# A fused LoRA, attention and mixture kernel on one core: x first among the loads, zero products in waits, adapter products in half-height tiles, the last tile in two parts

## The reference, cut to what matters

```python
# 1: dense layer with a LoRA adapter (rank 16) chosen by sequence; * 2.0
base_out = jnp.einsum('bti,oi->bto', x, W) + b
lora_h = jnp.einsum('bti,bir->btr', x, lora_As[adapter_mapping])
y = base_out + jnp.einsum('btr,bro->bto', lora_h, lora_Bs[adapter_mapping]) * SCALING
# 2: attention, 32 query heads of 16 on 8 key/value groups, rotary, causal
q, k, v = y @ Wq, y @ Wk, y @ Wv            # split in heads
q, k = _apply_rope(q, cos_t, sin_t), _apply_rope(k, cos_t, sin_t)
weights = jax.nn.softmax(jnp.where(causal, -jnp.inf, scores) / 4.0, axis=-1)
x1 = x + (weights_times_v @ Wo)             # the residual is added outside the layer
# 3: dense layer with a rank-32 adapter chosen by sequence (5 labels); * 0.5
z = x1 @ W2.T + (x1 @ A2[label]) @ lora_B_w.T * 0.5
# 4: mixture of 4 rank-16 experts, top 2 gates
gates = softmax over the two largest of z @ router_w.T
out = x1 + sum over experts of gate * ((z @ A.T) @ B) * 4
```

## Time and profile before

| | us |
|---|---|
| median of 3 runs (169.52 to 172.09) | 171.23 |
| the profiled execution's own time | 172.04 |
| its span, first to last instruction | 170.4 |
| TensorE busy | 146.8 (86%) |
| DVE, ACT, POOL busy | 96.2, 78.8, 76.7 |
| mean granted clock of TensorE | 0.984 |

### The profile page before, as it was taken

One profiled execution on the slowest core, in us unless ns is written; L12 is line 12 of the kernel. 1 busy time (PEld: TensorE's weight loads), 2 busy tenths in 40 slices (PEclk: granted clock), 3 DMA queues, 4 the chain that ended last, 5 costly groups with the idle time before them and its releaser, 6 DMA issues.

```text
span 170.4 us, 4660 instructions
## 1 busy us (share of the span) xinstructions
PE 146.8 (86%) x1792; PEld 126.9 (74%) x1792; DVE 96.2 (56%) x215; ACT 78.8 (46%) x158; POOL 76.7 (45%) x78
## 2 busy tenths in 40 slices
PE   0049899999898998999999998999999899888942
PEld 0048749988887996888899996888997778666620
DVE  0045265170559853545829872676964388756583
ACT  2235072794246987133347961215498341833110
POOL 0360054039694999226221684447209845720000
PEclk9999999999999999999999999999999999999985
DMA  5998867632122201224302361002432100623114
GB/s 169 287 294 241 349 251 258 229 65 59 46 81 61 65 2 44 58 64 133 100 0 81 119 199 61 0 0 89 144 119 102 65 0 2 188 100 129 37 62 185
DMA packets 15143, 19.32 MB, mean 113 GB/s; under 512 B 5714, under 2 KB 10066, under 8 KB 14866
## 3 DMA queue, kind: packets, MB, share of 16 engines
q1 hardware_dynamic: 14146, 16.94, 30.5%
q10 hardware_dynamic: 720, 1.84, 3.3%
q0 software_dynamic: 256, 0.26, 0.6%
HBM read 12.47 MB, written 2.10 MB: 86 GB/s over the span
## 4 chain that ended last, share of the span: by engine, by line
PE 49%; POOL 17%; ACT 12%; DVE 9%; DMA 6%; issue 4%; SPq 1%; POOLq 1%; DVEq 0%
PE bank L928 34%; PE bank L954 7%; DMA xF<-xt 6%; ACT qx L302 5%; POOL ex L514 5%; PE bank L983 4%; PE bank L936 4%; POOL qr L545 3%; POOL Kbd L551 2%; POOL qkc L526 2%; POOL kr L539 2%; ACT kx L302 2%; POOL sm L519 1%; POOL qks L533 1%; DVE cTl L676 1%
## 5 line engine op out<-in xcount | busy, mean ns | idle before, releaser
L519 POOL TENSOR_TENSOR sm<-sm,mx 128x512 f32<-128x512 f32 x16 | 17.1, 1073 | 25.1 <-DVE mx L699 24.9
L954 PE MATMUL bank<-xTh,WTh 128*128 128x256 f32 x64 | 16.9, 304 | 10.9 <-ACT xTh L302 10.9
L514 POOL TENSOR_TENSOR ex<-ex,ri 128x512 f32<-128x512 f32 x16 | 17.7, 1106 | 13.1 <-DVE ri L705 13.1
L302 ACT COPY qx<-bank 32x512 f32<-32x512 f32 x32 | 18.5, 577 | 5.7 <-PE bank L928 5.3
L954 PEld LDWEIGHTS bank<-xTh,WTh 128*128 128x128 f32 x64 | 11.8, 205 | 11.3 <-issue 11.0
L694 DVE TENSOR_TENSOR sm<-bank,mixed 128x512 f32<-128x512 f32 x16 | 10.6, 675 | 16.6 <-PE bank L928 16.6
L368 ACT ACTIVATE ex<-sm 128x512 f32<-128x512 f32 x16 | 10.2, 635 | 18.7 <-POOL sm L519 18.5
L928 PE MATMUL bank<-yTh,Wqh 128*128 128x256 f32 x64 | 18.3, 285 | 0.0
L928 PE MATMUL bank<-yTh,Wql 128*128 128x256 f32 x64 | 17.9, 280 | 0.0
L928 PE MATMUL bank<-yTl,Wqh 128*128 128x256 f32 x64 | 17.9, 280 | 0.0
L954 PE MATMUL bank<-xTl,WTh 128*128 128x256 f32 x64 | 16.6, 293 | 0.4 <-DVE xTl L643 0.4
(11 more groups left out here) (97 smaller groups left out, 364.1 us busy)
## 6 DMA issues: line engine op xcount, KB each, us to landing
RS<-RL SPq DMA_DIRECT2D x32, 136.0 KB, 2.0
xF<-xt SPq DMA_DIRECT2D x8, 256.0 KB, 6.2
xres<-xn SPq DMA_DIRECT2D x8, 256.0 KB, 3.2
out<-x SPq DMA_DIRECT2D x8, 256.0 KB, 2.1
Wqn<-wq ACTq DMA_DIRECT2D x2, 512.0 KB, 9.4
Wn<-w SPq DMA_DIRECT2D x1, 1024.0 KB, 4.9
Wqn<-wo SPq DMA_DIRECT2D x1, 1024.0 KB, 4.8
x<-small SPq DMA_DIRECT2D x1, 904.0 KB, 6.9
```

What stands on the lines that cost most here:

```text
L302: return nc.scalar.copy(dst, src)
L514: nc.gpsimd.tensor_tensor(ex[:, j], ex[:, j], ri[:, j, :, None].broadcast_to((P, 2 * NG, T)), ALU.mult).then_inc(normed, 1)
L519: nc.gpsimd.tensor_tensor(sm[:, j % 2], sm[:, j % 2], mx[:, j, :, None].broadcast_to((P, 2 * NG, T)), ALU.subtract).then_inc(shifted, 1)
L954: nc.tensor.matmul(FR[c // 2][:, (c % 2) * TOK:(c % 2 + 1) * TOK], WT[u][:, k, P * c:P * (c + 1)], xT[r][:, k], start=first, stop=False, s ...
```

## The change

What it does, in the order of the kernel:

- **Loads.** Half 0 of x is SP's first transfer, before `mix`; half 1 follows `mix`. `ids` is loaded by POOL. ACT loads W blocks 0, 1, 2; it issues the halves of Wq later, between its casts (the first after `w_high(1)`, the second after `wq_high(0)`). W2 and Wkv are issued ahead of `small` (the router and label weights), and the tables for group 1 (`next_slots(1)`) and 2 directly behind Wo; `load_x(3)` stands ahead of `load_x(2)`, and both behind `next_slots(2)`.
- **First product.** `y_first` goes by contraction block k: the high products of block k as soon as it is there, the low ones (`y_first_low`) a step later; `adapter_in(0)` stands ahead of the last low block.
- **Folding.** `fold_router` and `fold_label_b` stand behind three q tiles and a kv tile, no longer ahead of them.
- **Zero products.** `keep_clock(n, dst)` is n float32 products of a 128x128 tile of zeros (`still`, set by DVE) with itself: 10 ahead of the first product, 6 between `y_adapter` and the first q tile, 6 near the end. Nothing reads them.
- **Adapter output.** `hT` is block-diagonal: rows 0 to 63 have values only in token columns 0 to 127, rows 64 to 127 only in columns 128 to 255. `y_adapter` now makes 8 products of 64 rows and 128 columns where it made 4 of 128 rows and 256 columns. Products that follow each other take the two halves of the rows in turn and write to two banks; between the two calls stands a wait on the new semaphore `y_half`, and `y_ps` is counted in the second call only.
- **Last tile in two parts.** For the last token tile `project_cols` makes columns 0 to 255 and 256 to 511 of the projection in two banks, each followed by its own `last_residual`, `last_transposes` and `last_cols`.
- **Orders.** Most of the lists on ACT, POOL, DVE and TensorE are written anew.

The core of the diff (the lists of calls cut to a few lines):

```diff
+            def load_x_half(g, h):
+                sp.dma_start(xF[g % 2][:, 2 * h:2 * h + 2], xt[g, :, 2 * h:2 * h + 2]).then_inc(d_x[g % 2][h], 16)
...
+            load_x_half(0, 0)
             load_mix()
-            load_ids()
+            load_x_half(0, 1)
             load_w(3)
-            load_x(0)
             first_slots()
...
+            next_slots(1)
+            next_slots(2)
+            load_x(3)
             load_x(2)
...
+            def last_cols(half, src):
+                act.wait_ge(x1T_ps, TT * G + half)
+                copy(flat(x1T[:, 1, 2 * half:2 * half + 2]), src[:, 0:D // 2]).then_inc(x1T_sb, 1)
...
+            def last_residual(half, src):
+                dve.wait_ge(wo_ps, TT * G + half)
+                cols = slice(D // 2 * half, D // 2 * (half + 1))
+                V.tensor_tensor(x1[:, 1, 1, cols], src[:, 0:D // 2], xres[:, 1, cols], ALU.add).then_inc(x1_sb, 1)
...
+            def keep_clock(n, dst):
+                pe.wait_ge(blank, 1)
+                for _ in range(n):
+                    mm(dst[:, 0:P], still[:], still[:], True, True)
...
             def y_adapter(g, h):
-                pe.wait_ge(h_sb, g + 1)
-                for c in (2 * h, 2 * h + 1):
-                    dst = FR[h][:, (c % 2) * TOK:(c % 2 + 1) * TOK]
-                    i = nc.tensor.matmul(dst, B1[g % 2][:, P * c:P * (c + 1)], hT[:], start=False, stop=True, skip_group_check=True)
-                i.then_inc(y_ps, 1)
+                if h:
+                    pe.wait_ge(y_half, g + 1)
+                else:
+                    pe.wait_ge(h_sb, g + 1)
+                for n in range(2):
+                    for e in ((1, 0) if h else (0, 1)):
+                        rows, b = slice(P // 2 * e, P // 2 * (e + 1)), e ^ h
+                        i = nc.tensor.matmul(FR[b][:, n * TOK + P * e:n * TOK + P * (e + 1)],
+                                             B1[g % 2][rows, P * (2 * b + n):P * (2 * b + n + 1)], hT[rows, P * e:P * (e + 1)],
+                                             start=False, stop=True, skip_group_check=True)
+                        if h and n:
+                            i.then_inc(y_ps, 1)
+                if h == 0:
+                    i.then_inc(y_half, 1)
...
+            def project_cols(half, dst):
+                pe.wait_ge(cT_l, 2 * G)
+                cols = slice(D // 2 * half, D // 2 * (half + 1))
+                for h in range(PH):
+                    i = mm3(dst[:, 0:D // 2], [c[:, h, SEQ // 2:SEQ].rearrange("p s t -> p (s t)") for c in cT],
+                            [w[:, h, cols] for w in Wo], h == 0, h == PH - 1)
+                i.then_inc(wo_ps, 1)
...
+            keep_clock(10, ZB)
             y_first(0)
             y_first(1)
+            y_first_low(0)
+            y_first(2)
+            y_first_low(1)
+            y_first(3)
+            y_first_low(2)
             adapter_in(0)
+            y_first_low(3)
             y_adapter(0, 0)
             y_adapter(0, 1)
+            keep_clock(6, ZB)
```

More of the change, by code:

```diff
@@ L122, in program @@
         Wkvn = x1T[:].rearrange("p t (k n) m -> p (t k) n m", n=2)
+        still = sb("still", [P, P])
         mid = sb("mid", [P, TT, EW])
@@ L389, in mgT_copy @@
                 copy(mgT[:, ts], src[:, 2 * P:4 * P].rearrange("p (t n) -> p t n", t=TT)[:, ts]).then_inc(mgT_h, ts.stop - ts.start)
+            load_w(0)
+            load_w(1)
             load_w(2)
[L392 to L393 removed]
+            x_high(0, 0)
+            w_high(0)
+            w_high(1)
             load_wq(0)
+            x_high(0, 1)
+            w_high(2)
+            w_high(3)
+            wq_high(0)
             load_wq(1)
[L396 to L401 removed]
             wq_high(1)
[L403 removed]
+            load_exp()
+            wq_high(2)
+            wq_high(3)
             y_high(0, 0)
[L405 removed]
             y_high(0, 1)
[L407 removed]
+            q_swap(0, 0)
+            rtt_copy()
+            wo_high(0)
             x_high(1, 0)
[L409 to L411 removed]
             q_swap(0, 1)
             kv_copy(0)
+            rl_copy(0, ZB)
+            k_swap(0)
             b_high()
[L415 to L419 removed]
             rl_copy(1, YB)
+            x_high(1, 1)
             v_copy(0)
@@ L446, in _ @@
             y_high(2, 0)
+            exp(1, 0)
+            y_high(2, 1)
             exp(1, 1)
-            y_high(2, 1)
             x_high(3, 0)
-            x_high(3, 1)
             x1_cols(0, 0, XB)
             x1_cols(0, 1, YB)
+            gate_exp(0, slice(0, TT))
             pt_copy(1, 0, ZB)
+            pt_copy(1, 1, YB)
             exp(1, 2)
-            pt_copy(1, 1, YB)
-            gate_exp(0, slice(0, TT))
+            kv_copy(2)
+            k_swap(2)
+            mgT_copy(0, slice(0, TT), XB)
+            x_high(3, 1)
+            ctx_high(1, 0, ZB)
             q_swap(2, 0)
-            kv_copy(2)
-            mgT_copy(0, slice(0, TT), XB)
-            k_swap(2)
-            ctx_high(1, 0, ZB)
             exp(1, 3)
@@ L625, in _ @@
             k_blocks(3, 0)
+            q_sum(3, 1)
             k_blocks(3, 1)
@@ L1080, in project, with last_transposes @@
                     i.then_inc(wo_ps, 1)
+            def project_cols(half, dst):
[5 more added lines that the diff above has]
+                i.then_inc(wo_ps, 1)
+            def last_transposes(half, dst):
+                pe.wait_ge(x1_sb, TT * G + half)
+                for k in range(2):
+                    i = tr(dst[:, P * k:P * (k + 1)], x1[:, 1, 1, P * (2 * half + k):P * (2 * half + k + 1)])
+                i.then_inc(x1T_ps, 1)
             def x1_transposes(g, t, dst):
```

392 lines of the change are left out of this document (188 added, 204 removed).

## The result

The changed kernel takes 175.96 us (median of 4 runs, 174.55 to 176.36); the kernel before took 170.53 beside it (median of 4). The ratio is 1.032, with a 95% interval of 1.022 to 1.042: 3.2% slower, where 3.3% faster was forecast. The profiled execution took 176.36 us with a span of 174.6, against 170.4 before.

What follows compares the result with a forecast made beforehand. It took the kernel as bound by loads and casts at the start, TensorE in the middle, and engine-to-engine steps in the tail. Six terms summed to -5.7 us: 171.2 to 165.5 us (span 164.7), 3.3% faster, range 162.3 to 169.6.

Steps and rivals of the forecast that it cites:

- Term 1: Start: first q product at 20.0 instead of 26.48, -6.5 us (bounds -6.9 and -4.3).
- the first rival: Start: adapter loads still need 6 us and the q tiles begin at the lower clock; 169.6 us, chance 0.12.
- the start doesn't pay: Another name for the first rival, on late adapter loads and a lower clock: 169.6 us, chance 0.12.
- Term 2: Folding: no longer in the wait for y_low, it stands among the q tiles, operands not late; +4.2 us.
- Term 3: Up to the scores of group 0: TensorE reaches scores(0, 0) as POOL ends the k path; -0.6 us.
- Term 4: Adapter output: half-height pairs run together, 1.4 us instead of 1.81, 0.4 less in three groups; -1.2 us.
- Term 5: Middle, groups 1 to 3: same TensorE products, no new wait of size; 0 us (bounds -2.8 and +3).
- the third rival: Groups 0 to 2: softmax transposes cause new waits on POOL, 0.67 us for each of twelve tiles; 172.7 us, chance 0.08.
- Term 6: Tail: last tile in two parts ends 1.2 us earlier, zero products' clock gives 0.4; -1.6 us.

Runs made afterwards that it cites:

- e3: The kernel before with ids issued by POOL instead of SP, nothing else changed: 173.64 us in one run.
- e1: The changed kernel with ids issued by SP behind half 0 of x, no longer by POOL: 172.90 us, ratio 1.003 to the kernel before.
- e11: e5 without the ten zero products at the start and the six ahead of the q tiles: 173.19 us, ratio 1.016 to the kernel before.
- e9: e5 with the adapter output in whole tiles, as in the kernel before: ratio 1.006 to the kernel before.
- e2: The changed kernel with 28 more zero products ahead of adapter_in(0): 174.01 us, ratio 1.010 to the kernel before.
- e15: e13 with the adapter output in whole tiles, as in the kernel before: ratio 0.989 to the kernel before, span 167.2 us.
- e5: The changed kernel with ids on SP behind half 0 of x and 18 more zero products ahead of adapter_in(0): 170.60 us, ratio 0.991 to the kernel before.
- e6: e5 with small loaded ahead of W2 and the folding ahead of the q tiles instead of six zero products: 173.82 us, ratio 0.999 to the kernel before.
- e7: The kernel before with the last tile in two parts, in the changed kernel's order of last calls, without zero products: 172.88 us, ratio 0.999.
- e13: The changed kernel with ids as SP's first transfer and six zero products ahead of the first adapter_in: 170.47 us, ratio 0.9875 to the kernel before.
- e14: e13 with Wkv ahead of W2 and small ahead of b and x of group 1 on SP: 169.98 us, ratio 0.988 to the kernel before.
- e10: The kernel before with the last tile in two parts and six zero products ahead of delta(2, 1): 172.7 us, ratio 1.013.
- e12: e9 with ids as SP's first transfer, ahead of half 0 of x: 171.03 us, ratio 1.0035 to the kernel before.

## Why the prediction was wrong

**Term 1, the start (-6.5 forecast, +0.7 measured), is the step that failed**, and in it the sentence on the adapters: "`ids` comes 0.4 us earlier now, so 10.4", with the landing at 13.1, at worst 16.4. The last load was issued at 13.03 and landed at 18.7.
- I compared when `ids` is issued, not who issues it, and not what lies ahead of it. Even the issue was not 0.4 us earlier: it was at 1.42, where 1.33 was. By POOL it takes 2.2 us more than before until the numbers can be read (6.0 for 3.8; e3 has the same), and with SP behind half 0 of x it would still be 0.8 more (e1). The profile before had no small load by POOL at a start, so the cost should have stood with a bound; it had none.
- The landing, taken at 2.7 us beside Wq, was too short as well: loads issued near 10.4 took 3.1 to 4.1 us (e11, e9, the changed kernel), so even on time the last would have come 0.4 to 1.4 us later than 13.1.
- "At that time only Wq is on its way" held for a load at 10.4. Shifted to 13.03 it fell behind W2, which I had expected at 12.5 and which came at 12.61. The two estimates stood a few lines apart and were not tried against a later load. Issued 2.6 us later than forecast, it took 5.7 us instead of 2.7, and so came 5.6 late.
- The clock was in the first rival, but only for the q tiles and for a landing 6 us late. It fell in the wait ahead of `adapter_in(0)`, which with the base products done at 12.0 and a landing at 13.1 would have been 1.1 us, and was 6.8. It cost 2.1 us (e2). The six zeros behind were at a clock already lost.
- With `ids` first on SP and zeros in the wait the term comes out at -7.6 (e15). From `adapter_in` to the first q product I had 6.9 us and it is 5.6: Wq's second half lands at 13.8, not at 16.2, so its casts don't end last. The rival "the start doesn't pay" had the right mechanism at half its size: 4.1 us over the forecast, where the changed kernel lost 7.2 until the first q product and 0.7 behind it.

**Term 2, the folding (+4.2)**: right. It is 4.2 in the changed kernel and in the versions that fold there, and the net gain of the start is what is left over it. Its operands weren't late.

**Term 3 (-0.6)** had the wrong sign: `scores(0, 0)` waits 1.32 us for `Kbd` where 0.57 was, +0.75, in e5, e9 and e15 alike. POOL's queue is the late one, not TensorE. In e6, with the folding ahead of the q tiles, the wait is 0.56, so this loss seems to belong to the folding's new place as well; e6 changed other things too.

**Term 4 (-1.2)**: right in mechanism, mis-sized: -0.9 in groups 1 to 3 (1.3 gained in the middle, 0.4 lost in group 1), and -0.5 with the 0.4 that group 0 loses, which the forecast didn't have. I had measured the duration of the products and said of `y_ps` at the end that other products lie over it in groups 1 to 3; in group 1 none do. The output itself took 1.50 us for 1.4 forecast, stop at `y_half` and both changes of mode included, so the drain that the Trainium skill names ("TensorEngine Tiling (Array Packing)", Key Properties) is not a whole record each time here.

**Term 5 (0)**: right to half a microsecond; with whole tiles the middle is 97.1 us as before (97.17), though a set of transposes has left it. None of the waits on `ex` that the third rival needed came (0.9 us in all).

**Term 6 (-1.6)**: -1.3, right within its bounds, but for the tail alone it needs the label loads in time, which I hadn't named (e7: with the wait for them and the lower clock the tail gains nothing).

The best versions here, e13 to e15, are 1.1 to 1.25% under the kernel before, with intervals that reach from 0.977 to 0.998. The span of e15, 167.2, is 2.5 over my 164.7: -1.1 in term 1; +2.6 up to group 1 (`Kbd` 0.75 and the 0.6 not had, the moved transposes 0.6, Wkv 0.24, whole tiles 0.4); +0.75 in the middle and +0.3 in the tail.

## What to carry to other kernels

Look for the load on whose values other loads depend, and give it the first place on the fastest issuer, ahead of any large one: 0.45 us earlier in issue was 2.2 us in reading its numbers, since half of x no longer lay ahead of it, and 2.5 us at the last of sixteen transfers. When a start is shortened, draw its transfers in order of issue with the large ones marked, and ask for each small one what happens if it slips behind one. And put zero products where the new wait will be, not where the old one was, counted so that they end with the load and not after it.

## What the chip showed that I hadn't expected

- A load of 0.2 KB issued by POOL took 4.6 us to land at the start (the page's row below), and the adapter loads behind it could start 1.4 us (e1) or 2.2 us (e3) later than with SP as issuer. The Trainium skill ("DMA: Bandwidth & Descriptors", Specifications) gives a first byte after about 1 us on POOL's path and 0.6 on SP's; the differences here are three to six times as large. It isn't a cost of every load of POOL: of the adapter loads of the changed kernel issued from 8.60 to 10.2, POOL's took 2.2 and 2.3 us and SP's 1.9 to 2.1. Why the first one is so late stays open.

```profile
Wn<-w SPq DMA_DIRECT2D x1, 1024.0 KB, 6.8
...
ids<-idt POOLq DMA_DIRECT2D x1, 0.2 KB, 4.6
```

- A transfer of 32 KB lands after 1.8 to 2.4 us in a quiet queue, after 3.8 to 4.1 beside half of Wq, 5.7 behind W2 and 8.1 behind `small`, whichever engine's queue the large one was issued on. The order of landing isn't that of issue: the adapter load of 13.03 landed at 18.7, W2, issued at 12.61, at 19.4.
- VectorE's step on two SBUF inputs (a low part, 0.69 us) takes 1.3 to 2.0 us beside a POOL step that reads SBUF (2.66 for two in e14, 4.88 for three in the changed kernel, 4.02 for two in e10), and `y_low`, with one input in PSUM, does not (four in 1.66 us beside the low part of Wkv in e2). In e9 even a step of 128x32 took 2.30 us for 0.18: it began at 21.18 beside POOL's low part of Wkv and ended at 23.48, with it (23.44). That agrees with the Trainium skill ("SBUF — State Buffer", SBUF: two separate sides), by which of such a pair the one that starts first locks the shared ports for its whole instruction and the other waits.
- The granted clock fell in or just behind waits that no zeros covered and came back 3.4 us (e3, e11) to 13.7 us (the changed kernel) later; it fell behind a wait of 2.77 us ahead of the q tiles (e11), not behind one of 2.32 with zeros ahead of it (e14). The start isn't the same twice: the first eight base products took 1.25 us in e12 and 2.07 in e13, with the same ten zeros ahead of them, and the trace gives the granted clock as 1.00 for both.
